# The four engine loops of an attention block: four steps per round in place of two

## The reference

```
h = layernorm(x) * (1 + ca) + sa
x = x + ga * attention(h)          # gated delta rule, 16 key heads, 32 value heads of 128
h = layernorm(x) * (1 + cb) + sb
x = x + gb * experts(h)            # 2 of 6 experts for each sample
```

```
T = solve_triangular(eye - A, eye);  value_ = T @ v_beta;  k_cumdecay = T @ (k_beta * exp(g))
v_new = v_i - kcd_i @ state
out_i = (q_i * exp(g_i)) @ state + attn @ v_new
new_state = state * exp(g_last) + (k_i * exp(g_last - g_i)).T @ v_new
```

## Time and profile before

| what | value |
|---|---|
| median of 3 runs | 5353.44 us (5352.12 to 5354.04) |
| the profiled execution's own time | 5352.04 us |
| its span, first to last instruction | 5350.3 us |
| mean granted TensorE clock | 0.987 of full |
| busy share PE / DVE / ACT / POOL | 93% / 84% / 82% / 39% |
| DMA, mean share of 16 engines on the data queue | 21.8% |
| instructions fetched, queue 8 and queue 14 | 0.33 MB and 0.47 MB |

### The profile page before, as it was taken

The page is one execution under the profiler, slowest core; times in us unless marked ns, Lnnn a source line. Parts: engine busy times, 40 slices in busy tenths (PEclk is TensorE's granted clock), DMA queues, the critical chain, the costliest instruction groups (busy, mean ns, idle before and its releaser), DMA issues. The chain is left out here.

```text
span 5350.3 us, 132947 instructions
## 1 busy us (share of the span) xinstructions
PE 4982.9 (93%) x38788; PEld 3326.6 (62%) x38788; DVE 4483.8 (84%) x9152; ACT 4371.8 (82%) x9744; POOL 2064.9 (39%) x1433
## 2 busy tenths in 40 slices
PE   5899999999999999999999999999999999999978
PEld 3566666666666666666666666666666666666644
DVE  4888888888888888888888888888888888888853
ACT  3788888888888888888888888888888888888842
POOL 2344434344443434444344444434444343444410
PEclk7999999999999999999999999999999999999988
DMA  3222212121121212212121221212122121221112
GB/s 141 75 63 63 75 62 81 60 70 69 62 81 60 79 60 72 71 62 77 60 82 61 65 74 62 81 59 74 65 66 77 60 79 60 72 70 62 64 65 82
DMA packets 185165, 377.26 MB, mean 71 GB/s; under 512 B 86400, under 2 KB 95744, under 8 KB 184960
## 3 DMA queue, kind: packets, MB, share of 16 engines
q1 hardware_dynamic: 185088, 376.46, 21.8%
HBM read 360.13 MB, written 16.25 MB: 70 GB/s over the span
## 5 line engine op out<-in xcount | busy, mean ns | idle before, releaser
L653 PE MATMUL p_proj<-hid,w_in 128*128 128x512 f32 x3072 | 1620.5, 610 | 32.4 <-POOL ident L1163 29.7
L998 DVE SCALAR_TENSOR_TENSOR conv<-pre,taps,conv 128x512 f32<-128x512 f32 x1536 | 1207.8, 793 | 41.9 <-ACT conv L857 37.6
L911 ACT ACTIVATE x_bd<-x_t 64x512 bf16<-64x512 bf16 x1280 | 804.5, 629 | 215.7 <-DVE x_t L1079 198.9
L1205 POOL TENSOR_TENSOR o_sc<-o_sc,neg_half 128x8 f32<-128x8 f32 x128 | 268.6, 2099 | 1622.0 <-DVE o_sc L1135 1622.0
L653 PEld LDWEIGHTS p_proj<-hid,w_in 128*128 128x128 f32 x3072 | 496.6, 192 | 64.5 <-POOL ident L1163 30.0
L838 PE MATMUL p_out<-h_t,w_out 128*128 128x512 f32 x1024 | 501.9, 613 | 0.8 <-DVE h_t L1140 0.8
L1072 DVE TENSOR_TENSOR y_h<-p_lev,y_h 128x512 bf16<-128x512 f32 x640 | 441.3, 690 | 44.2 <-PE p_lev L707 37.9
L1116 DVE TENSOR_TENSOR vw<-p_b,w_c 128x256 f32<-128x256 f32 x384 | 156.9, 409 | 378.8 <-PE p_b L796 378.8
L1079 DVE STREAM_TRANSPOSE x_t<-y_h 128x512 bf16<-128x512 bf16 x640 | 454.6, 710 | 19.3
L1064 DVE TENSOR_TENSOR q_h<-p_lev,consts 128x512 bf16<-128x512 f32 x640 | 438.6, 685 | 37.9 <-PE p_lev L701 33.3
L1172 POOL TENSOR_TENSOR low<-g_row,consts 128x1024 f32<-128x1024 f32 x128 | 302.1, 2360 | 410.1 <-ACT dec L895 409.9
(11 more groups left out here) (210 smaller groups left out, 12168.4 us busy)
## 6 DMA issues: line engine op xcount, KB each, us to landing
w_in<-in_w_in SPq DMA_DIRECT2D x128, 768.0 KB, 6.2
g_row<-rows_scratch SPq DMA_DIRECT2D x128, 512.0 KB, 3.1
hid<-h_scratch SPq DMA_DIRECT2D x128, 512.0 KB, 7.3
e_row<-exp_rows_scratch SPq DMA_DIRECT2D x128, 512.0 KB, 5.1
w_out<-in_w_out SPq DMA_DIRECT2D x128, 256.5 KB, 2.6
x<-in_x SPq DMA_DIRECT2D x8, 512.0 KB, 10.4
h_scratch<-x SPq DMA_DIRECT2D x8, 512.0 KB, 2.6
y_scratch<-y_acc SPq DMA_DIRECT2D x8, 512.0 KB, 5.6
```

The lines of the kernel that those rows point to most:

```text
L653: last = pe.matmul(p_proj[tile % 2][:], w_in[p][:, kt, tile * P:(tile + 1) * P], hid[p][:, kt, :], start=(kt == 0), stop=(kt == KT - 1))
L911: last = act.activation(x_bd[block, :, block], x_t[block], ACT.Copy)
L998: dve.scalar_tensor_tensor(conv[:, tile, :], pre[:, tile, j:j + S], taps[p][:, tile, j:j + 1], conv[:, tile, :], ALU.mult, ALU.add).then_i ...
```

## The change

A round of the hardware loop of each compute engine holds four iterations in place of two. The number of rounds goes from 62 to 31, so that the loop covers the same iterations 0 to 123, and the written-out iterations before and behind it are the same. The counter's multiples in the steps' numbers and in the counts of loads are adapted. Orders, waits, buffers and SP's program are as before.

```diff
@@ -463,7 +463,7 @@
-        SPARE = 3
+        SPARE, TURN = 3, 4
@@ -511,11 +511,11 @@
         def loop(eng, emit, order):
             for iteration in range(-LEAD, 0):
                 run(eng, emit, order, fixed(iteration))
-            rounds = (NIT - LEAD) // 2
+            rounds = (NIT - LEAD) // TURN
             with eng.Fori(0, rounds) as m:
-                for u in range(2):
-                    run(eng, emit, order, lambda off: Step(m * 2 + (u + off), (u + off) % 2, m + (u + off) // 2))
-            for iteration in range(rounds * 2, NIT):
+                for u in range(TURN):
+                    run(eng, emit, order, lambda off: Step(m * TURN + (u + off), (u + off) % 2, m * (TURN // 2) + (u + off) // 2))
+            for iteration in range(rounds * TURN, NIT):
                 run(eng, emit, order, fixed(iteration))
```

## The result

| | before | after |
|---|---|---|
| median of 4 runs | 5352.94 us (5352.12 to 5354.04) | 5390.35 us (5383.94 to 5395.71) |
| the profiled execution's own time | 5352.04 us | 5387.1 us |
| its span | 5350.3 us | 5385.3 us |

The ratio is 1.0069 with a 95% interval of 1.0052 to 1.0087: 37 us slower. The forecast of "slower" and its range hold, its 5416 us is 26 us too high, so it took the loss for 63 us where it was 37.

The account below looks back on a forecast made before the run. Bound: the 128-step attention loop, where every engine waits for every other. 30 x (2.0 for PE + 0.9 for ScalarE) = 87 us more, 24 us less register work: +63 us, so 5416 us; range 5340 to 5500 us.

Parts of the forecast that it names:

- What bounds the kernel, and the gain: Attention loop: every engine waits for others; 31 first-of-a-round steps lose register work, 0.78 us each, 24 us less.
- PE's miss: PE's closing branch: doubled loop code isn't kept and is fetched again; 2.0 us exposed at each of 30 taken branches.
- The choice of 4.1 us for the stall: PE's closing branch: next instruction 4.1 us later on a miss, between SP's median and its worst.
- The cover of 2.3 us: PE's closing branch: the array still works off queued matmuls for 2.3 us, which hides that much of the stall.
- ScalarE's miss: ScalarE's closing branch: at SP's median 3.7 us, L951 starts 0.9 us late, on top of PE's exposed time.
- VectorE and GpSimd: Closing branches: VectorE misses, hidden behind its 3.16 us wait for PE; GpSimd's 116 instructions fit; neither costs anything.
- The clock: Sign of being right: PE's clock still full.
- B: Rival, closing branches: PE's loop still fits, ScalarE and VectorE miss; +3 us, 5356 us; chance 0.12.
- C: Rival, closing branches: nothing misses, as compute engines keep more code than SP; 5329 us; chance 0.14.
- D: Rival, closings: no cover, misses delaying each other, or a second fetch; 30 x 8.5 - 24, 5584 us; chance 0.10.
- The traffic of code: DMA queues: 30 rounds of some 20 packets (11 of 16 KB, 10 of 8 KB), 8 MB beside 377 MB; no cost.

## Why the prediction was right, and where its sum was off

**What bounds the kernel, and the gain: right.** Of the steps 39.48 us long 31 are gone, and the second and third step of a round take 38.7 us, as those with constants did. The cause named is register work. PE's sequencer in the second and third step of a round of after, as in the earlier trace rows:

```profile
L483 PEldq ALU_OP  x16: 32/32/32, 1681.9 to 1709.3; - x16
L483 PEldq FUSED_REGOPS  x5: 37/37/37, 1687.1 to 1700.2; - x5
...
L483 PEldq ALU_OP  x16: 32/32/36, 1720.6 to 1750.1; - x16
L483 PEldq FUSED_REGOPS  x5: 37/37/37, 1725.6 to 1738.9; - x5
```

Five FUSED_REGOPS where a first step has 12. It is not the time of the branches: that grew from 0.3 us to 2.4 us and more on three engines, and 24 of 30 first steps still take 39.5 to 39.6. The kernel that computes none has no 39.48 us steps at all, and the two that change one side only divide the 0.78 us: 0.28 with PE's part left, 0.61 with the others'. They don't add up to 0.78, so a little of each lies beside the other, and the text was right to count the four engines' work once.

**PE's miss: right in kind, its term of 60 us (30 x 2.0) was 50 (30 x 1.66).** That PE misses at all was taken over from SP; no row of before showed where PE's limit lies, and it could have gone the other way. The choice of 4.1 us for the stall, because PE's packets are twice as large, was the error; the median was 3.6 us, close to SP's median of 3.7. The cover of 2.3 us was right: the branch at 1633.9, the end of L838 at 1636.21. With 3.6 in place of 4.1 the step gives 1.5 us, and the mean of 30 gives 1.66.

**ScalarE's miss: a term of 27 us (30 x 0.9) that was nothing.** The step "at SP's median 3.7 us the table load starts 1.4 us late" took one engine's stall for another's. ScalarE's was 2.4 us, and its Exps were queued for 2.3 us. The kernel with PE at two steps shows it by itself: ScalarE stalls at 30 closings, and no step is longer for it.

**VectorE and GpSimd: right.** VectorE's stall is as long as forecast (4.0 against 3.7 us) and lies in a wait of 3.17 us for PE that begins after its queued work; the same kernel shows that it costs nothing. GpSimd's loop, 112 instructions in the trace, is kept (0.25 us to the next instruction).

**The clock: forecast as "still full", wrong.** It fell in six of 30 rounds and cost 11.6 us. So the sum is 50 + 0 + 12 - 24 = +37 where 60 + 27 - 24 = +63 was forecast: two terms 37 us too high, one of 12 us missing. That the forecast came within 26 us is in part luck, since the missing term took back a third of the error.

**The rivals.** B (PE's loop fits) fell with the branch of 3444 ns and would have shown 20 packets on queue 8. C (nothing misses) is what the hint makes of the kernel: 5336 us against its 5329. D (8.5 us a closing) fell with the longest step, 42.97 us, in a round of lower clock. The traffic of code, 12 packets a round on queue 8 where 11 were forecast and 13 on queue 14 where 10 were, costs little, as said: with the hint nearly all of it is still there and at most 7 us with it.

## What to carry to other kernels

Before a loop is made longer, count for each engine the instructions between two of its closing branches, and find in the same trace a loop that is kept and one that isn't; a loop that crosses that line pays a stall at every closing, and what it costs is the stall less the work that is queued in the engine at its branch, so what decides is by how much an engine's stall exceeds its cover: PE and ScalarE both had 2.3 us of work queued and stalled 3.6 and 2.4 us, and VectorE, with the longest stall of the three (4.0 us), cost nothing. Read the stall from the branch to the next instruction, not from the branch's own row. If the loop must be that long, a hint to fetch the branch's target ahead takes the stall away, for 5 to 7 us once where the loop is left (here 30 or 14 stalls saved); and where waits compare with values computed from a counter, the steps written out with constants were the fastest here (5307 us), at the price of 7.7 MB of instructions fetched.

## What was not expected of the hardware

- **The clock falls after a short stall.** In after, the array stood idle for 1.4 to 2.4 us at each closing. Six times the clock then fell to half; all six stood behind an idle stretch of 1.68 us or more. It is no sure sign: 12 of the 30 were that long, the second longest (1.96 us) without a fall. With PE alone at four steps seven falls came, with eight steps a round three; without PE's stall (before, the others alone, either hint, no loop) none inside the loop. With eight steps and the hint it fell once just behind the loop, 1.6 us after the idle stretch of 1.91 us shown above. So a stall of 1.66 us had a second price of 0.39 us on the mean. Whether it also makes the runs differ more is not shown: ten runs with eight steps lie 20 us apart, but 13 of the kernel before 12 us.
- **Stalls differ by engine**: 3.3 to 4.3 us on PE, 3.3 to 5.0 on VectorE, 2.4 to 2.7 on ScalarE, 2.9 to 4.1 on GpSimd, 3.5 to 4.5 on SP. In after each of PE's 30 holds one packet of queue 8: it starts 0.9 to 1.5 us after the branch and takes 0.9 to 1.8 us, and the next instruction comes 1.4 to 1.6 us after its end. So what varies is the fetch, and the rest of the stall is nearly fixed.
- **More is fetched than the loop holds.** The kernel without a loop fetched 5.29 MB for PE's 82755 instructions, 64 bytes each, so a packet of 16 KB is 256 of them and one of 8 KB is 128. 378 instructions are 3.0 blocks of 128 and bring 5 packets a round, 448 are 3.5 and bring 6, PE's 2645 are 10.3 blocks of 256 and bring 12. An estimate from these: depending on where a loop begins in its first block, this is one or two blocks more than it touches on GpSimd, and none or one on PE. What they hold, no run shows.
